# Cross-attention in a fused layer: key sums, query norms and scores in four column groups of 32 instead of two of 64

## What is computed

```
q = layernorm(x) @ Wq                 # 64 queries x 128
k = ctx @ Wk                          # 64 keys x 128
q = q * rsqrt(mean(q*q) + 1e-5) * gq  # a norm for each query
k = k * rsqrt(mean(k*k) + 1e-5) * gk  # a norm for each key
scores = (q @ k.T) / sqrt(128)        # 64 x 64
attn = softmax(scores);  out = attn @ v;  out @ Wo
```

## Time and profile before

| | us |
|---|---|
| median of 3 runs | 674.62 |
| lowest and highest run | 674.62, 675.5 |
| the profiled execution's own time | 675.08 |
| its span | 673.3 |
| TensorE matmuls busy | 662.0 (98% of the span) |
| TensorE weight loads busy | 579.1 (86%) |
| DVE busy | 451.8 (67%) |
| ACT busy | 327.7 (49%) |
| POOL busy | 249.3 (37%) |
| granted TensorE clock, mean | 0.999 |

### The profile page before, as it was taken

How to read it: one execution, slowest core, us unless ns; L and a number is a source line. 1 busy time by engine, 2 the same in 40 slices (tenths; PEclk the granted TensorE clock), 3 DMA queues, 4 the chain that set the end, 5 groups by cost and what they waited for, 6 DMA issues and landing times.

```text
span 673.3 us, 14521 instructions
## 1 busy us (share of the span) xinstructions
PE 662.0 (98%) x5412; PEld 579.1 (86%) x5412; DVE 451.8 (67%) x885; ACT 327.7 (49%) x657; POOL 249.3 (37%) x337
## 2 busy tenths in 40 slices
PE   7999999999999999999999999999999999999997
PEld 5788888888888889989998989988887878888886
DVE  4777775786865777585677678746557777655555
ACT  5756656667653344343344333354465444444443
POOL 2321121121223343334333345416544455555553
PEclk9999999999999999999999999999999999999999
DMA  6513112011011212322222222103332223333332
GB/s 210 182 48 95 48 49 72 25 39 35 24 33 48 63 64 67 96 65 75 79 64 63 63 64 64 38 27 94 93 94 79 81 85 87 93 93 93 93 93 95
DMA packets 35865, 50.07 MB, mean 74 GB/s; under 512 B 4064, under 2 KB 22880, under 8 KB 35808
## 3 DMA queue, kind: packets, MB, share of 16 engines
q1 hardware_dynamic: 35376, 48.89, 24.6%
q10 hardware_dynamic: 432, 0.39, 0.2%
HBM read 48.22 MB, written 1.05 MB: 73 GB/s over the span
## 4 chain that ended last, share of the span: by engine, by line
PE 90%; DVE 4%; ACT 2%; issue 1%; DMA 1%; POOL 0%; SPq 0%; DVEq 0%; ACTq 0%
PE acc L546 22%; PE bank_k L519 15%; PE bank_q L519 15%; PE bank_v L519 7%; PE bank_v L622 7%; PE bank_s L666 5%; PE bank_s L519 4%; PE bank_p L687 2%; PE bank_p L652 2%; PE bank_p L697 2%; PE bank_t L697 2%; PE bank_t L674 2%; PE bank_q L643 2%; PE bank_k L632 1%; ACT pv_hi L984 1%
## 5 line engine op out<-in xcount | busy, mean ns | idle before, releaser
L546 PE MATMUL acc<-wo_hi,pv_hi 128*128 128x256 f32 x328 | 94.3, 287 | 0.2 <-DVE pv_lo L1332 0.2
L546 PE MATMUL acc<-wo_lo,pv_hi 128*128 128x256 f32 x328 | 92.7, 283 | 0.0
L546 PE MATMUL acc<-wo_hi,pv_lo 128*128 128x256 f32 x328 | 92.1, 281 | 0.0
L1468 POOL TENSOR_TENSOR wq_lo<-raw_a,wq_hi 128x256 fp32r<-128x256 f32 x32 | 24.1, 753 | 144.3 <-DVE wq_hi L1269 144.3
L1468 POOL TENSOR_TENSOR wq_lo<-raw_m,wq_hi 128x256 fp32r<-128x256 f32 x50 | 41.7, 834 | 72.4 <-DVE wq_hi L1288 68.2
L905 ACT ACTIVATE kt<-bank_k 128x512 f32<-128x512 f32 x64 | 38.4, 600 | 60.8 <-PE bank_k L519 60.8
L546 PEld LDWEIGHTS acc<-wo_hi,pv_hi 128*128 128x128 f32 x328 | 61.5, 188 | 3.4 <-issue 0.4
L1332 DVE TENSOR_TENSOR pv_lo<-rows_t,pv_hi 128x512 fp32r<-128x512 f32 (+1 forms) x51 | 39.0, 766 | 38.0 <-ACT pv_hi L984 38.0
L546 PEld LDWEIGHTS acc<-wo_lo,pv_hi 128*128 128x128 f32 x328 | 61.8, 188 | 1.9
L546 PEld LDWEIGHTS acc<-wo_hi,pv_lo 128*128 128x128 f32 x328 | 62.0, 189 | 0.0
L519 PE MATMUL bank_q<-xt_hi,wq_hi 128*128 128x512 f32 x146 | 59.7, 409 | 1.6 <-POOL wq_lo L1468 1.0
(11 more groups left out here) (196 smaller groups left out, 1902.7 us busy)
## 6 DMA issues: line engine op xcount, KB each, us to landing
raw_m<-in_chunk_m SPq DMA_DIRECT2D x50, 256.0 KB, 2.7
raw_a<-in_head_a SPq DMA_DIRECT2D x48, 192.0 KB, 2.6
raw_b<-in_head_b SPq DMA_DIRECT2D x32, 256.0 KB, 3.0
raw_m<-in_chunk_m SPq DMA_DIRECT2D x50, 128.0 KB, 2.1
raw_v<-in_pair_v SPq DMA_DIRECT2D x16, 256.0 KB, 2.8
raw_b<-in_head_b SPq DMA_DIRECT2D x32, 128.0 KB, 2.1
xs<-in_x SPq DMA_DIRECT2D x6, 128.0 KB, 3.2
out<-xs SPq DMA_DIRECT2D x3, 256.0 KB, 2.4
```

The lines of the kernel that those rows point to most:

```text
L546: last = nc.tensor.matmul(acc[t // 2][:, (t % 2) * D:(t % 2 + 1) * D], w[:, tok], m, start=begins and n == 0, stop=True, skip_group_check= ...
L1468: nc.gpsimd.tensor_tensor(lo, raw, hi, ALU.subtract).then_inc(signal, 1)
```

## The change

The three products are cut in blocks of 32 output partitions, so that consecutive calls go to four groups of 32 columns of the array. `ones_of` shrinks to 32 columns. `norm_k` has four calls in place of two, with the same 512 moving columns each. `norm_q` has 32 calls in place of 16. `scores` has 32 in place of 16 for the stage "a"; in stage "b" its width stays 64. Results, their places and all semaphores stay the same.

```diff
+GROUP = 32
...
-        ones, ones_of = sb("ones", [P, 1]), sb("ones_of", [P, SEQ])
+        ones, ones_of = sb("ones", [P, 1]), sb("ones_of", [P, GROUP])
...
                 for h in range(2):
-                    for b in range(NS):
-                        t, s = divmod(b, SPB)
-                        last = nc.tensor.matmul(bank_q[s * SEQ:(s + 1) * SEQ, h * NT + t:h * NT + t + 1],
-                                                sq_q[:, h, b * SEQ:(b + 1) * SEQ], ones[:], start=True, stop=True)
+                    for b in range(HT // GROUP):
+                        t, j = divmod(b, P // GROUP)
+                        last = nc.tensor.matmul(bank_q[j * GROUP:(j + 1) * GROUP, h * NT + t:h * NT + t + 1],
+                                                sq_q[:, h, b * GROUP:(b + 1) * GROUP], ones[:], start=True, stop=True)
...
                 for s in range(SPB):
                     keys = sq_k[:].rearrange("p h (t s k) -> p (h t) s k", s=SPB, k=SEQ)[:, :, s, :]
-                    last = nc.tensor.matmul(bank_p[s * SEQ:(s + 1) * SEQ, :], ones_of[:], keys, start=True, stop=True)
+                    for j in range(s * SEQ, (s + 1) * SEQ, GROUP):
+                        last = nc.tensor.matmul(bank_p[j:j + GROUP, :], ones_of[:], keys, start=True, stop=True)
...
-                        last = nc.tensor.matmul(bank_s[s * SEQ:(s + 1) * SEQ, g * SEQ:(g + 1) * SEQ], qt[:, h, tok],
-                                                kt[:, h, tok], start=True, stop=True)
+                        width = GROUP if u.kind == "a" else SEQ
+                        for j in range(0, SEQ, width):
+                            last = nc.tensor.matmul(bank_s[s * SEQ + j:s * SEQ + j + width, g * SEQ:(g + 1) * SEQ],
+                                                    qt[:, h, at + j:at + j + width], kt[:, h, tok], start=True, stop=True)
```

## The result

The changed kernel takes 677.42 us (677.0 to 679.0) against 674.75 us (674.62 to 675.5) for the kernel before on the same chip: a ratio of 1.0042, 95% interval 1.0027 to 1.0057. It is slower by about 0.4%, where 669.2 had been forecast. The profiled execution of the changed kernel took 677.13 us, its span 675.3.

The account below looks back on a forecast made before the run. TensorE's own instruction stream was taken to bound the 16 cross-attention pairs. norm_q -0.38, scores +0.05 and norm_k -0.01 make -0.34 us a pair, x 16 = -5.4 us: 669.2 us against the 674.62 median, range 666 to 677.

Parts of the forecast that it names:

- the block's sum: norm_k, norm_q and scores of one cross-attention pair: -0.38 + 0.05 - 0.01 = -0.34 us, taken 16 times.
- a round of four: norm_q's four loads of 32 columns, one per group: 35 ns a round taken, 16 rounds in 0.56 us instead of 0.94.
- A change of width between the products: Between norm_k, norm_q and scores: converting all three together avoids two more load-engine stops, up to 0.34 us a pair.
- The softmax chain: DVE's work behind the scores: with scores 0.34 us earlier, 0.24 us of room remains, so the gain stays.
- Rivals 1: Cross-attention products: a load gets no cheaper below 64 columns, a round stays 58.7 ns; 675.4 us, chance 0.10.
- Rivals 1 and 2: The second, in the cross-attention products: only two of four groups run at once; +30.6 us, 705.2 us, chance 0.09.
- rival 3: TensorE's norm_q and scores: a least price per load and matmul makes both double; +30.6 us, 705.2 us, chance 0.09.
- Nothing else is late next: After the cross-attention products: no other engine takes the gain of 0.34 us a pair away.
- the smaller `ones_of` counts for nothing: Memset at the start: half its width saves some 0.05 us at most, hidden by the data's arrival; nothing counted.
- The rule on the floor of matmul starts: TensorE: matmul starts never under about 25 ns apart; as an average, an estimate of +21 us, 0.03 of 0.09 chance.

Follow-up runs that it names:

- run 1: Changed kernel with the later stages' weights loaded in pairs 4 to 8 instead of ahead of pair 2: 673.34 us, ratio 0.9977 to the kernel before.
- run 2: Changed kernel, but the first two pairs keep two groups of 64 and `ones_of` its 64 columns: 671.13 us, ratio 0.9939 to the kernel before.
- run 5: Changed kernel plus 32 useless one-column calls (128 more instructions) on TensorE before its first product: 672.92 us, ratio 0.9968 to the kernel before.
- run 10: Changed kernel, but only the first pair keeps two groups, with `ones_of` at 64 columns: 670.36 us, ratio 0.9932 to the kernel before.
- run 4: Changed kernel with the scores back in two groups, norm_k and norm_q in four: 673.04 us, ratio 0.9968 to the kernel before.
- run 9: Changed kernel with norms in four groups, scores in two, and `ones_of` allocated with 64 columns: 672.02 us, ratio 0.9954 to the kernel before.
- run 7: Kernel before, same instructions, with every buffer behind `ones_of` moved by 128 bytes by a pad: 676.82 us, ratio 1.0027 to the kernel before.
- run 6: Changed kernel with `ones_of` allocated with 64 columns but only 32 used, so addresses stay: 675.11 us, ratio 1.0004 to the kernel before.
- run 8: Changed kernel with late loads of later weights, 128 added instructions and `ones_of` allocated with 64 columns: 672.0 us, ratio 0.9954 to the kernel before.

## Why the prediction was wrong

These parts were right: TensorE's stream bounds the cross-attention, four groups run at once, and the block's sum is -0.34 us. That the sum came out exactly is luck, since its errors cancel. Inside it norm_q was over-rated (-0.29 measured, -0.38 forecast; a round of four takes 39 ns, not 35), and the scores and norm_k were under-rated (-0.03 each where +0.05 and -0.01 stood). The sum was also taken 16 times, and 15 pairs gained. A change of width between the products was put at up to 0.17 us and costs 0.10. The softmax chain did not take the gain away. Rivals 1 and 2 are out by this alone, and so is rival 3 as it was priced, with a least price for every load and matmul: the 64 matmuls of norm_q start within 0.58 us, 9 ns apart on average, each with its load.

**The step that failed** is "Nothing else is late next". It looked at the engines and their semaphores and left out the stream of instructions as a supply. Rival 3 had the right resource, but as a steady rate that decides from 14.9 ns an instruction pair. What the runs show is a supply in blocks of 256: TensorE used the 272 loads and matmuls of norm_k, norm_q and the scores in 2.5 us where it had used 136 in 2.9, and where the end of a block fell right behind them it stood still for 2.69 us. That cost 2.7 us for the stop, and 1.5 us for the half clock behind it (runs 1, 2, 5, 10). The Trainium skill, "Runtime: NRT & Kernel Launch", section "Instruction fetch mechanics", says that the instruction memory is refilled in blocks of 16 KB, 256 instructions, and that this is mostly hidden. The packets of 16 KB and the remainder of 193 agree with the first; the 2.69 us do not with the second.

**A second step** that failed was that the smaller `ones_of` counts for nothing. It was costed as a memset alone. As a buffer it moved everything behind it by 128 bytes, and that costs 1.2 us by the stretches of the trace. By the times it is 1.0 us (run 4 against run 9), 1.9 us (run 7) or 2.3 us (the changed kernel against run 6); which is right stays open.

The account of the spans: 15 blocks at -0.34 make -5.1 us; the stop +2.7; the half clock +1.5; the addresses +1.2; the smaller stop +0.3. These make +0.6, and +2.0 was measured. Of the 1.4 us that remain, 0.4 us stand ahead of the first pair (its norm_k starts at 16.36 us instead of 15.95); the rest was not taken apart.

The rule on the floor of matmul starts, in the Trainium skill's "TensorE: Matmul & The Clock Gate", section "Wait — 56ns, not 53.3ns?", does not hold over several column groups: the 9 ns above are far below its 25. The part of rival 3's chance that stood on it went to a rule that does not bind here.

## What to carry to other kernels

Splitting small matmuls in narrower column groups gives its gain where the weight load sets the pace (norm_q, -0.29 us a pair) and next to none where the stream does (the scores, -0.03). It pays in instructions: count how many of them a dense stretch needs, and look where the blocks of 256 end and how busy the DMA engines are there. A stop named "issue" inside a product, without a semaphore, can be this. Moving the block's end by making other code shorter or longer is a test and, as runs 5 and 10 show, a cure, though blocks can then end at another bad place (run 8). And when a change resizes a buffer, keep the addresses of the others if only its effect is to be judged.

## What was not expected of the hardware

- A layout moved by 128 bytes in every partition lengthens the experts' work by 40 ns per two chunks (8.40 to 8.44 us), with the same instructions in the same order.
- With the DMA engines 32% busy (24 to 32 us) a block of instructions still came 1.3 us too late; with them at 83 to 85%, 2.7 to 3.2 us.
- After each of eight such stops TensorE went on 1.4 to 1.55 us behind the end of the last packet of the instruction queue, whatever the traffic.
- One stop of 2.7 us with TensorE busy for 0.48 us of it was followed by 3.4 us at 1.2 GHz; one of 1.3 us was not, and one of 3.2 us by 6.8 us of it, which began before the stop ended.
